# Attention scores computed once: a new order for softmax and its transposes in a gated cross-attention kernel

## What is computed

```python
# cross-attention with a tanh gate (x is layer-normed twice on the way in)
q = (xn @ w_q).reshape(B, 256, 16, 64)
k, v = jnp.split(context @ w_kv, 2, axis=-1)             # each [B, 512, 16, 64]
scores = jnp.einsum('bqhd,bkhd->bhqk', q * SCALE, k)
attn = jax.nn.softmax(scores, axis=-1)
out = jnp.einsum('bhqk,bkhd->bqhd', attn, v).reshape(B, 256, 1024) @ w_out + b_out
x = x + tanh(g_xattn) * out * tanh(gate)
# top-1 mixture of 8 experts with room for 160 tokens each, on the layer-normed x
logits = tokens @ gate_w; expert_idx = argmax(softmax(logits))
x = x + tanh(g_ffn) * combine(relu(expert_input @ w1) @ w2)
```

## Time and profile before

| | before |
|---|---|
| median of runs | 590.01 us |
| the profiled execution's own time | 591.27 us |
| its span, first to last instruction | 589.4 us |
| mean granted TensorE clock | 0.973 |
| TensorE / VectorE / ScalarE / GpSimd busy | 510.6 / 411.6 / 359.9 / 327.5 us |
| one steady batch (8 pairs) | 66.6 us |
| bytes moved by DMA | 16.18 MB, mean 27 GB/s |

### The profile page before, as it was taken

One profiled execution on the slowest core, in us unless ns is written; L12 is line 12 of the kernel. 1 busy time (PEld: TensorE's weight loads), 2 busy tenths in 40 slices (PEclk: granted clock), 3 DMA queues, 4 the chain that ended last, 5 costly groups with the idle time before them and its releaser, 6 DMA issues.

```text
span 589.4 us, 15522 instructions
## 1 busy us (share of the span) xinstructions
PE 510.6 (87%) x6476; PEld 422.9 (72%) x6476; DVE 411.6 (70%) x762; ACT 359.9 (61%) x483; POOL 327.5 (56%) x209
## 2 busy tenths in 40 slices
PE   5789999998898999998898989998898999986294
PEld 3577878776786778776786768776786778775194
DVE  5887786777957776777857786777867775884112
ACT  5667775776656665676656665676656765662041
POOL 4655664555655565465655565465645565564115
PEclk9999999999999989999999999999999999998588
DMA  7800000600000000000000000000000000000201
GB/s 206 281 2 21 1 3 6 166 2 11 11 10 20 2 19 2 28 3 3 18 11 19 3 17 3 28 2 2 14 11 1 2 7 3 10 1 13 85 10 42
DMA packets 19541, 16.18 MB, mean 27 GB/s; under 512 B 2163, under 2 KB 16931, under 8 KB 19472
## 3 DMA queue, kind: packets, MB, share of 16 engines
q1 hardware_dynamic: 18096, 11.88, 6.9%
q0 software_dynamic: 1376, 3.30, 1.5%
HBM read 10.83 MB, written 5.14 MB: 27 GB/s over the span
## 4 chain that ended last, share of the span: by engine, by line
PE 59%; DVE 24%; ACT 7%; issue 7%; DMA 2%; POOL 1%; POOLq 0%; SPq 0%; DVEq 0%
DVE MX L720 7%; PE psAB L926 6%; PE psEF L989 6%; DVE VL L710 5%; PE psO L1051 4%; PE psO L1053 4%; PE psX L1110 4%; PE psO L1052 4%; PE psCD L1030 4%; PE psAB L928 4%; PE psAB L927 4%; ACT VH L562 3%; PE psCD L1025 3%; DVE HL L704 2%; ACT HL L551 2%
## 5 line engine op out<-in xcount | busy, mean ns | idle before, releaser
L495 POOL TENSOR_TENSOR PARTS<-P,PARTS 128x1024 f16<-128x1024 f32 x128 | 274.2, 2145 | 191.5 <-DVE PARTS L728 146.9
L720 DVE TENSOR_REDUCE MX<-psEF 128x2 f32<-128x1024 f32 x128 | 156.3, 1221 | 0.8 <-PE psEF L989 0.4
L1051 PE MATMUL psO<-VH,PARTS 128*128 128x65 f16 x1024 | 100.6, 195 | 0.2 <-DVE winners L794 0.2
L1052 PE MATMUL psO<-VL,PARTS 128*128 128x64 f16 x1024 | 99.9, 193 | 0.0
L1053 PE MATMUL psO<-VH,PARTS 128*128 128x65 f16 x1024 | 99.7, 194 | 0.0
L704 DVE TENSOR_TENSOR HL<-psAB,HL 128x768 fp32r<-128x768 f32 x63 | 60.3, 958 | 53.9 <-ACT HL L551 53.9
L587 ACT ACTIVATE P<-psAB,lift 128x1024 f32<-128x1024 f32 x64 | 71.3, 1114 | 42.3 <-PE psAB L1030 39.2
L1051 PEld LDWEIGHTS psO<-VH,PARTS 128*128 128x128 f16 x1024 | 92.6, 98 | 3.3 <-DVE winners L794 0.3
L1052 PEld LDWEIGHTS psO<-VL,PARTS 128*128 128x128 f16 x1024 | 93.5, 99 | 0.0
L1053 PEld LDWEIGHTS psO<-VH,PARTS 128*128 128x128 f16 x1024 | 93.5, 97 | 0.0
L989 PE MATMUL psEF<-HL 64*128 64x512 f32 x256 | 63.9, 495 | 33.7 <-DVE MX L720 32.3
(11 more groups left out here) (179 smaller groups left out, 899.9 us busy)
## 6 DMA issues: line engine op xcount, KB each, us to landing
ctx_raw<-in_ctx_dram SPq DMA_DIRECT2D x8, 256.0 KB, 2.9
w1s<-in_L_ffn_w_dram SPq DMA_DIRECT2D x8, 256.0 KB, 5.2
w2s<-in_L_ffn_w_dram SPq DMA_DIRECT2D x8, 256.0 KB, 4.7
experts_table<-zeros POOLq DMA_DIRECT2D x2, 645.0 KB
PARTS<-experts_table SPq DMA_DIRECT2D x2, 516.0 KB, 4.3
wraw<-in_L_xattn_w_kv_dram SPq DMA_DIRECT2D x4, 256.0 KB, 4.6
out_dram<-row SPq DMA_DIRECT2D x8, 128.0 KB, 1.8
X<-in_x_dram SPq DMA_DIRECT2D x1, 896.0 KB, 8.3
```

What stands on the lines that cost most here:

```text
L495: pool.tensor_tensor(PLO[:, par, :, cols], P32[:, par, :, cols], PHI[:, par, :, cols], ALU.subtract).then_inc(plo_done, 1)
L720: dve.tensor_reduce(maxima, psEF2, AX.X, ALU.max, negate=True).then_inc(max_done, 1)
L1051: pe.matmul(psO[:, g:g + DH + 1], phi, VH[:, kt, head, 0:DH + 1], start=first_, stop=False)
L1052: pe.matmul(psO[:, g:g + DH], phi, VL[:, kt, head, :], start=False, stop=False)
```

## The change

The scores are computed once, queries by keys: for each of two query tiles qt one bank pair ([128 queries, 2 heads x 512 keys]). VectorE takes the maximum of those finished scores, a second small instruction scales it by SCALE and adds LIFT, and the result NB is the per-partition bias of the exponential. One exponential covers one head, so there are four for a pair. The float16 parts then have queries on the partitions; the DMA transposes them, one transfer for each query tile with high and low part of both heads ([128, 2048] to PT [128, 16, 128]), issued from SP. `values` reads PT and runs two slots behind. The maximum pass, its transposes, NM and the bias matmuls are gone. Key/query and value projections all use psEF and take turns in it; the steps of the surrounding work and the order within a slot are rearranged on every engine.

```diff
-        P32 = sb("P32", [P, 2, 2, KT * SQ], F32)
-        PARTS = sb("PARTS", [P, 2, 2, 2, KT * SQ], F16)
+        P32 = sb("P32", [P, 2, QT, 2 * SK], F32)
+        PARTS = sb("PARTS", [P, 2, QT, 2, 2 * SK], F16)
+        PT = sb("PT", [P, 2, QT, 2, 2, KT, P], F16)
...
-        PROJECT_STEP = 2
-        CTX_STEP = KT - 1
+        def transposed_value(j):
+            return 16 * (j // 2 + 1)
+        PROJECT_STEP = 3
+        CTX_STEP = 1
+        VALUES_BEHIND = 2
...
-            return psCD if j == 1 else psAB
+            return psCD if j == 1 else psEF
-        def score_bank(c):
-            return psCD if c else psAB
+        def score_bank(qt):
+            return psCD if qt else psAB
-        psV = psCD[:, 0:512]
+        psV = psEF[:, 0:512]
-        MOMENTS_STEP, TOK_STEP, TOKT_STEP, LOGITS_STEP, RANKS_STEP = 3, 4, 5, 6, 7
+        MOMENTS_STEP, TOK_STEP, TOKT_STEP, LOGITS_STEP, RANKS_STEP = 4, 5, 5, 6, 7
```

SP's queue, whole:

```diff
+            def transpose_parts(j, qt):
+                par = j % 2
+                sp.wait_ge(plo_done, 2 * j + qt + 1)
+                if j >= 2 and qt == 0:
+                    sp.wait_ge(pv_done, j - 1)
+                sp.dma_start_transpose(PT[:, par, qt].rearrange("p s h k n -> p (s h k) n"),
+                                       PARTS[:, par, qt].rearrange("p s n -> p (s n)")).then_inc(pt_in[qt][par], 16)
             def batch(b):
+                for j, hp in slots(b):
+                    if hp == 0 and b == 1:
+                        for e in range(E):
+                            sp.dma_start(w2s[:, e], w2[e].rearrange("(c p) d -> p c d", p=P)).then_inc(w2_in, 16)
+                    if is_first(b) and hp:
+                        sp.dma_start(w1s[:, hp, :], w1[hp]).then_inc(exp_w_in, 16)
+                    if hp == CTX_STEP + 1 and b + 2 < B:
+                        sp.wait_ge(ctxt_psum, b + 2)
+                        sp.dma_start(ctx_raw[:], ctx_t[b + 2]).then_inc(ctx_in, 16)
+                    for qt in range(QT):
+                        transpose_parts(j, qt)
+                    if hp == MOMENTS_STEP and not is_first(b):
+                        x1_store(b - 1)
```

GpSimd's residual:

```diff
+                        pool.wait_ge(phi_done[qt], j + 1)
+                        if j >= 2:
+                            pool.wait_ge(pt_in[qt][par], transposed_value(j - 2))
+                        pool.tensor_tensor(PARTS[:, par, qt, 1], P32[:, par, qt], PARTS[:, par, qt, 0],
                                            ALU.subtract).then_inc(plo_done, 1)
```

ScalarE's exponentials:

```diff
+                act.wait_ge(bias_done, 2 * j + qt + 1)
+                if j >= 2:
+                    act.wait_ge(plo_done, 2 * j - 4 + qt + 1)
+                for h in range(2):
+                    last = act.activation(P32[:, par, qt, SK * h:SK * h + SK], score_bank(qt)[:, SK * h:SK * h + SK],
+                                          ACT.Exp, bias=NB[:, par, qt, h:h + 1], scale=SCALE)
```

VectorE's maximum and bias:

```diff
+                dve.wait_ge(score_psum, 2 * j + qt + 1)
+                dve.tensor_reduce(MX[:, par, qt, :], score_bank(qt)[:].rearrange("p (h n) -> p h n", h=2), AX.X, ALU.max,
+                                  negate=True).then_inc(max_done, 1)
+                dve.wait_ge(max_done, 2 * j + qt + 1)
+                dve.tensor_scalar(NB[:, par, qt, :], MX[:, par, qt, :], SCALE, LIFT, ALU.mult, ALU.add)\
+                   .then_inc(bias_done, 1)
```

TensorE:

```diff
             def k_project(b, hp):
-                    pe.wait_ge(exp_done, 2 * (j - AHEAD) + 1)
+                    pe.wait_ge(kq_lo_done, j)
+                    for free_when in ef_free:
+                        pe.wait_ge(*free_when)
...
             def v_project(b, half, kt, bank=psV, behind=None):
-                    pe.wait_ge(exp_done, after_exp)
+                    pe.wait_ge(kq_lo_done, min(behind + 1, B * PAIRS))
+                    ef_free.append(v_free)
...
+            def scores(b, hp, qt):
+                    pe.wait_ge(kq_lo_done, j + 1)
+                if j:
+                    pe.wait_ge(exp_done, 2 * j - 2 + qt + 1)
+                for k, q in ((H_KHI, H_QHI), (H_KLO, H_QHI), (H_KHI, H_QLO)):
+                    for h in range(2):
+                        rows = slice(64 * h, 64 * h + 64)
+                        last = pe.matmul(score_bank(qt)[:, SK * h:SK * h + SK], hl[rows, q + P * qt:q + P * qt + P],
+                                         hl[rows, k:k + SK], start=(q == H_QHI and k == H_KHI), stop=(q == H_QLO))
...
             def values(b, hp):
+                for qt in range(QT):
+                    pe.wait_ge(pt_in[qt][par], transposed_value(j))
```

More of the change, by code:

```diff
@@ L391, in _ @@
             sp.dma_start(gw[:], gate_w).then_inc(exp_w_in, 16)
-            def batch(b):
[L394 to L404, removed]
+            sp.wait_ge(ctxt_psum, 1)
+            sp.dma_start(ctx_raw[:], ctx_t[1]).then_inc(ctx_in, 16)
+            sp.dma_start(w1s[:, 0, :], w1[0]).then_inc(exp_w_in, 16)
+            def transpose_parts(j, qt):
[5 more added lines that the diff above has]
+                                       PARTS[:, par, qt].rearrange("p s n -> p (s n)")).then_inc(pt_in[qt][par], 16)
+            def batch(b):
+                for j, hp in slots(b):
[11 more added lines that the diff above has]
+                        x1_store(b - 1)
             each_batch(batch)
@@ L636, in _ @@
             each_batch(batch)
+            ot_copy(B - 1, 2, psEF[:, 512:1024])
             ot_copy(B - 1, 3, FFN_BANKS[0])
@@ L873, in batch @@
                         ctxt_lo(b + 1)
+                    if hp == PROJECT_STEP and not is_first(b):
+                        add_attention(b - 1)
+                    if hp == MOMENTS_STEP and not is_first(b):
+                        token_moments(b - 1)
+                    if hp == TOK_STEP and not is_first(b):
+                        tokens(b - 1)
+                    if v_group(b, hp):
+                        v_lo(*v_group(b, hp))
                     if hp == LOGITS_STEP and not is_first(b):
@@ L884, in batch @@
                         dve.wait_ge(ident_zero, 4)
[L885 to L888 removed]
             each_batch(batch)
+            normalise_heads(B - 1, PAIRS - 2)
             normalise_heads(B - 1, PAIRS - 1)
@@ L980, in max_scores @@
                 if qt == 0:
-                    pe.wait_ge(kq_hi_done, j + 1)
-                    if j:
-                        pe.wait_ge(mrow_done, j)
-                else:
-                    pe.wait_ge(max_done, 2 * j + 1)
-                for h in range(2):
-                    rows = slice(64 * h, 64 * h + 64)
-                    last = pe.matmul(psEF[:, 512 * h:512 * h + SK], hl[rows, H_QHI + P * qt:H_QHI + P * qt + P],
-                                     hl[rows, H_KHI:H_KHI + SK], start=True, stop=True)
@@ L1072, in tok_transposes, with logits @@
                 last.then_inc(tokt_psum, 1)
-            def logits(b):
+            def logits(b, behind=None):
+                if behind is not None:
+                    pe.wait_ge(kq_lo_done, behind + 1)
+                    ef_free.append((route, b * ROUTE + 2))
                 pe.wait_ge(tokt_done, b + 1)
@@ L1175, in batch @@
                         project(b - 1)
+                    if hp == CTX_STEP and not is_last(b):
+                        ctx_transposes(b + 1)
+                    if j >= VALUES_BEHIND:
+                        values(*back(b, hp, VALUES_BEHIND))
                     if hp == TOKT_STEP and not is_first(b):
```

245 lines of the change are left out of this document (77 added, 168 removed).

## The result

The changed kernel takes 648.9 us (648.2 to 650.1, four runs) against 590.0 (589.0 to 590.9): ratio 1.100, interval 1.098 to 1.103. The forecast was 636, slower.

What follows compares the result with a forecast made beforehand. No engine was taken as full; the chain hops between engines. First batch +7, second +10, five at +6.8, last -2 (+50), XN's second wait -7, end +4.4, start -1: +46 on 590.0 gives 636 us, range 556 to 662.

Steps and rivals of the forecast that it cites:

- The mechanism: VectorE's small SBUF-only instructions wait for GpSimd's residuals over a shared port: 73.0 us a batch against 66.2 laid out before.
- TensorE's share: TensorE's work per pair of heads falls from 2.6 to 1.41 us, 9.5 us less a batch.
- Slot by slot: A batch's eight slots, each from a base of 6.1 to 6.2 us plus its waits, sum to 73.0 us.
- a rival (0.06): TensorE's clock falls to half rate; slot 3 alone gains 4 to 8 us: 665 us or more, chance 0.06.
- the forecast case: Collisions of VectorE with GpSimd's residuals make the kernel slower: 636 us, alone 608 to 662, chance 0.57.
- XN's second half: In slot 1 it waits 2.1 us behind the second residual but need not lose its turn; half was taken.
- The ends: First batch +7, last batch -2, uncovered transposes at the end +4.4, start -1 us.
- transfer rival: DMA transposes set the slot from 4.6 us each; at 5 us each 80 us a batch, over 700, chance 0.09.
- Removing the waits on NB and router alone leaves 66.8 a batch, no change: Argument against the faster rival: without the NB and router waits a batch would still take 66.8 us.
- The transposes at 0 in the loop: Two DMA transposes a pair fit under about 11 us of cover, so they add 0 to the loop.
- w2s ahead of pair 8: 0, under that cover: SP's eight w2s load issues, 5.3 us, stand ahead of pair 8's transposes and cost 0 under their cover.
- The collisions miss: Faster rival: with only xvv and XN waiting the loop falls 24 us, with none 40: 569 or 553, chance 0.25.

Runs made afterwards that it cites:

- a_short_residual: Changed kernel with GpSimd's residual of the probabilities cut to 2 columns, low parts zero: 543.1 us, ratio 0.920 to the kernel before.
- f_reordered: Changed kernel without NB, four VectorE blocks ahead of phi_first, router cut in two, ScalarE's value copy and TensorE's value projection earlier, context and x residuals later: 520.2 us.
- k_warm: Changed kernel plus 26 unread matmuls into unused columns of psO in slots 2 and 5, where TensorE idles: 637.4 us, ratio 1.077.
- g_router: Changed kernel without NB, with x moments, XN, token moments and tokens ahead of phi_first and the router's two halves cut apart: 531.4 us, ratio 0.901.
- h_double: Changed kernel with each DMA transpose issued twice, the copy into a spare buffer, SP waiting for the previous pair's transposes: 793.1 us, ratio 1.342.

## Why the prediction was right, and where it was off

- **The mechanism** held. NB, XN, vv, tokens and winners wait for GpSimd's residuals, and the wait turns a gain into a loss. With the residuals cut the batch is 58.1 to 59.8 us (58.5 laid out). The Trainium skill, SBUF — State Buffer, section Who interferes with whom, has this as an exclusive lock for the whole instruction; the ends that coincide within 0.1 us above agree.
- **TensorE's share** held: 9.5 us less a batch than 60.2 would leave 50.7 busy; a_short_residual has 50.1 at a clock of 0.97 in four steady batches and 51.6 at 0.94 in one, f_reordered 48.8 at 1.00. The mark "near 54" fits neither and had no row behind it; the 56.56 of the changed kernel is the same work at a clock of 0.86.
- **Slot by slot**, forecast to measured: 7.2 / 6.97, 10.5 / 9.96, 6.2 / 8.17, 8.5 / 8.62, 11.5 / 11.20, 9.6 / 10.60, 10.0 / 10.40, 9.5 / 9.16. The sum is 73.0 / 75.08. Slots 2 and 5 are 1.97 + 1.00 us over; the other six together are 0.9 under. These slots hold XN's second wait in full, of which the forecast took half, so it stood for 72.0 a batch and is 3.1 short.
- **The missing term is the clock.** It was a rival (0.06) that priced slot 3. The granted clock fell in slots 2 and 5 instead, behind the idles that the collisions make, so it comes on top of the forecast case, not in its place. k_warm's clean batch prices it at 2.7 us a batch, and slot 2 at a clock of 1.00 is then 6.23, the 6.2 of the forecast. Over the six batches behind the first that is about 16 us (an estimate, 6 x 2.7), against the 12.9 by which 636 fell short; k_warm as a whole gave 11.6 back.
- **XN's second half** "need not lose its turn": in the changed kernel it did. Both halves took 4.00 us against 0.68 unhindered, 3.3 of waiting where 1.7 + 1.05 was taken and 3.8 would have been the full price. That is 0.5 us a batch too little.
- **The ends** together were near: what lies outside the six batches from batch 1 on is 9.4 us longer, where +7 - 1 (half of XN's second wait) - 2 + 4.4 - 1 = +7.4 was forecast. The split was not as forecast, and it depends on where the batches are cut. By the second key residual of a batch the first batch takes 60.95 us after and 61.41 before, and the stretch from that point of the last batch to the end 126.5 and 116.4. By the first exponential of a batch the first is 3.6 us longer, that stretch 5.3, and the start 1.4 shorter. Neither gives the forecast's +6 for the first batch. What makes the end longer is not shown; the transposes are not it, since without them it is as long to 0.4 us. The six batches between are 7.9 to 8.6 us longer each, and they hold the miss: 49.6 us, where 10 + 5 x 6.8, less six halves of XN's second wait (6.3), makes 37.7.
- **The working** has slips of its own, all small. Slot 3's parts add up to 8.2 where 8.5 stands (8.62 measured), and slot 4's to 12.0 where 11.5 stands (11.20). The batches sum to +49, not +50. The transfer rival's 80 us a batch gives 636 + 8 x 7 = 692, not over 700. That the slots' errors, of both signs, leave only 2.1 us in the sum is in part luck.
- **NB** waited as laid out in slots 4 and 6 (1.30 and 0.94 us), and in slots 3 (1.30) and 1 (0.34) too; over the run that is (0.419 - 0.169) x 16 = 4.0 us a batch in busy time, where the layout had 2 x 1.2. The mark "mean well over 0.5 us" did not fit the forecast's own slots (1.2 + 1.2 over 16 instructions and the rest shorter) and was simply set wrong: the median is 0.170, the mean 0.419. "VectorE's chain share above TensorE's" did not come either: 30% to 33%.
- **"Removing the waits on NB and router alone leaves 66.8 a batch, no change"** was not run in that form. NB alone brings the batch to 69.6 to 72.1 us in the loop; NB, router and the four moved blocks (g_router) to 55.5 to 56.6.
- **The transposes at 0 in the loop** held: 0.03 us of 75. The rival's threshold of 4.6 us each was not reached at 2.78 or less; doubled, at 5.6, the batch was 89. The 4.4 us taken for the end did not show: 0.2 us in all between the kernel with and without them.
- **"w2s ahead of pair 8: 0, under that cover"** held only with the collisions in place: batch 1 took 75.9 against 74.8 to 75.1 later. In a_short_residual it took 67.2 against 58.1 to 59.8 later, and in f, with a batch of 54 us, spreading the loads gave 6.7 back.
- **The collisions miss** (569 or 553) is what a reached, at 543, though only by shortening the residuals. Its price was too small by the forecast's own layout: 66.2 - 58.5 = 7.7 us a batch is 62 over eight, where 40 was taken; in a the five steady batches are 6.7 to 9.0 us shorter than before.

## What to carry to other kernels

An instruction of 0.17 us can cost its neighbour's 2 us: before a small `tensor_scalar`, or one with two inputs in SBUF, goes on VectorE's critical loop, look at what GpSimd is in the middle of at that moment, and put it ahead of the step that releases GpSimd. Then read the waits again, because they move. Compare an instruction's mean with its shortest: 116 of VectorE's 516 busy us here were waiting. And judge a change apart from the collisions that its order makes: this one is 32 us faster with GpSimd's residuals cut in both kernels and 59 slower with them in.

## What the runs showed of the hardware that was not expected

- TensorE was busy in 56.6 of 75 us and still lost its clock behind single idles of 3.75 to 3.80 us. Start to start, 512 columns then take 0.42 us (320.82 to 321.24) against 0.24 (314.27 to 314.51), the 1.2 and 2.4 GHz levels. In a_short_residual the batch mean is 0.97 in four steady batches and 0.94 in one, in f_reordered 1.00.
- 26 matmuls that nobody reads, put into two such idles a batch, made the kernel 11.6 us faster (k_warm). In the batch where no wait of VectorE changed they were worth 2.7 us.
- XN's two halves, issued back to back, waited for two residuals. The first half did not carry the second through ahead of a GpSimd instruction that was ready by then (ScalarE's copy for it ended at 316.67, the residual before it at about 316.7). Where ScalarE's copy ended a little later and GpSimd was not ready (k_warm, 312.17 against 312.05), both halves went through after one residual, in 2.10 us.
- VectorE's `bn_stats`, with one input in SBUF, ran beside GpSimd's residual at its usual 0.28 us, while `tensor_scalar` of 128 x 2 waited for the end of it (vv at 308.54: 1.05 us against 0.17).
- A two-byte SBUF-to-SBUF transpose of 512 KB took at most 2.78 us of the queue, so at least 189 GB/s (524,288 bytes / 2.78 us), 4.4 us to landing, and 2.0 us of SP to issue (median, 1.3 to 6.0). The Trainium skill, DMA: Bandwidth & Descriptors, section Latency and other measured facts, gives 261 GB/s for one measured case; no run here reaches that rate, and h_double's, with a wait of its own in it, does not rule it out.
